# Sends over 128 partitions, the last three of them aimed past the table

## The reference, cut to what matters

```
h = (x @ W).reshape(n, 4, 64);  hl = sum(a_l * h);  hr = sum(a_r * h)
e = leaky_relu(hl[row] + hr[col]);  ee = exp(e - e_max[row])
att = ee / segment_sum(ee, row)[row];  out_h = segment_sum(att * h[col], row)       # row = src, col = dst
msgs = (x[src] @ rel_W[r]) where edge_type == r;  agg = segment_sum(msgs, dst)
out  = relu(x @ self_W + self_b + agg / deg)
```

## Time and profile before

| | |
|---|---|
| median of 3 runs | 1883.29 us (1882.06 to 1884.16) |
| span of the profiled execution, first to last instruction | 1879.7 us |
| PE, DVE, ACT, POOL busy | 76%, 66%, 32%, 70% of the span |
| sends of sort a (L761) | 102, 130.2 us busy |
| sends of sort b (L771) | 136, 167.7 us busy |
| gathers of both graph layers (L946) | 904, 862.2 us busy |

### The profile page before, as it was taken

How to read it: one execution, slowest core, us unless ns; L and a number is a source line. 1 busy time by engine, 2 the same in 40 slices (tenths; PEclk the granted TensorE clock), 3 DMA queues, 4 the chain that set the end, 5 groups by cost and what they waited for, 6 DMA issues and landing times.

```text
span 1879.7 us, 23044 instructions
## 1 busy us (share of the span) xinstructions
PE 1421.9 (76%) x6382; PEld 962.6 (51%) x6382; DVE 1234.0 (66%) x2879; ACT 608.8 (32%) x1757; POOL 1319.1 (70%) x1331
## 2 busy tenths in 40 slices
PE   5566567778888888679999966666666667786993
PEld 3333245655665555558876434444334333375992
DVE  6999977788898887868524125454444444477655
ACT  0688511136666665143332310000000000025435
POOL 0688677777777777768886747777777777714566
PEclk9799778889999999889999988988977776756996
DMA  5011144445544444310202574333333333305456
GB/s 98 10 30 32 19 106 108 107 104 134 143 121 118 122 117 107 107 44 10 58 2 66 140 227 114 107 105 106 106 104 106 105 106 106 104 26 147 149 154 187
DMA packets 110954, 186.08 MB, mean 99 GB/s; under 512 B 31578, under 2 KB 78125, under 8 KB 110701
## 3 DMA queue, kind: packets, MB, share of 16 engines
q0 software_dynamic: 56480, 134.84, 28.0%
q1 hardware_dynamic: 54349, 49.75, 9.4%
HBM read 152.80 MB, written 31.43 MB: 98 GB/s over the span
## 4 chain that ended last, share of the span: by engine, by line
POOL 37%; PE 23%; DVE 19%; issue 13%; DMA 8%; DVEq 0%; ACT 0%; POOLq 0%; SPq 0%; ACTq 0%
POOL gath L946 30%; PE ps L992 6%; DVE hot_c L675 6%; DMA gath<-y_tab,index_b 6%; POOL slot_tab_b L771 5%; PE ps L1482 4%; PE ps L1920 3%; PE ps L1931 3%; DVE hot_r L666 2%; DMA gath<-h_tab,index_a 2%; DVE acc L982 1%; DVE gath L1031 1%; PE ps L1656 1%; DVE hot L970 1%; POOL acc L1236 1%
## 5 line engine op out<-in xcount | busy, mean ns | idle before, releaser
L992 PE MATMUL ps<-gath,hot 128*125 128x260 f32 (+1 forms) x1808 | 595.4, 469 | 297.5 <-DVE gath L1031 99.1
L992 PEld LDWEIGHTS ps<-gath,hot 128*125 128x125 f32 x1808 | 364.3, 221 | 487.4 <-DMA gath<-y_tab,index_b 196.3
L946 POOL DMA_INDIRECT gath<-h_tab,index_a x464 | 446.2, 962 | 146.8 <-issue 136.2
L946 POOL DMA_INDIRECT gath<-y_tab,index_b x440 | 416.0, 945 | 154.9 <-issue 119.4
L982 DVE TENSOR_TENSOR acc<-acc,ps 125x257 f32 (+1 forms) x672 | 284.5, 423 | 316.6 <-PE ps L992 277.7
L716 PE MATMUL ps<-hot_c,pay 125*128 125x440 f16 (+1 forms) x901 | 194.6, 367 | 61.6 <-ACT pay L699 61.6
L771 POOL DMA_INDIRECT slot_tab_b<-sent_word_b,sent_to_b x136 | 167.7, 1233 | 36.3 <-issue 36.3
L761 POOL DMA_INDIRECT slot_tab<-sent_word,sent_to x102 | 130.2, 1277 | 81.7 <-DVE sent_to L514 50.9
L699 ACT ACTIVATE pay<-hot_r,plan_b 125x128 f16<-125x128 f16 x578 | 172.0, 386 | 0.0
L716 PEld LDWEIGHTS ps<-hot_c,pay 125*128 125x128 f16 x901 | 87.5, 100 | 160.6 <-ACT pay L699 81.5
L1031 DVE TENSOR_TENSOR gath<-gath,ps 128x1024 f32<-128x1024 f32 x116 | 136.0, 1214 | 0.0
(11 more groups left out here) (360 smaller groups left out, 2034.4 us busy)
## 6 DMA issues: line engine op xcount, KB each, us to landing
y_tab<-ybuf SPq DMA_DIRECT2D x25, 448.0 KB
y_slots<-y_buf SPq DMA_DIRECT2D x64, 128.0 KB, 1.9
gath<-h_tab,index_a POOLq DMA_INDIRECT x464, 2.8
gath<-y_tab,index_b POOLq DMA_INDIRECT x440, 2.8
h_tab<-hbuf SPq DMA_DIRECT2D x25, 113.8 KB
xa<-in_x SPq DMA_DIRECT2D x1, 2800.0 KB
xa<-in_x SPq DMA_DIRECT2D x5, 560.0 KB
xn_tab<-acc SPq DMA_DIRECT2D x5, 560.0 KB
```

The lines of the kernel that those rows point to most:

```text
L946: p.indirect_dma_start(gath[:, ring(k) + s, 0:width], None, table, bass.IndirectOffsetOnAxis(ap=index[g][:, col:col + 1], axis=0)).then_in ...
L992: ins = t.matmul(sum_p(g, q, width), hot[:, s, :], gath[:, s, 0:width], start=(e == 0), stop=(e == n - 1))
```

## The change

All four tiles get 128 partitions. Ahead of the first use GpSimd writes 0 over the words and 2^20 over the targets, in all 128 partitions; VectorE then fills partitions 0 to 124 as before, so that partitions 125 to 127 keep the target 2^20. Each send covers 128 partitions and carries a bound, the last index of its table (59391 or 56319). An index above the bound is skipped, without an error. The number of sends and their order stay.

```
+NOWHERE = 1 << 20
-    sent_word = low.tile("sent_word", [NP, SENT])
-    sent_to = low.tile("sent_to", [NP, SENT], I32)
+    sent_word = low.tile("sent_word", [128, SENT])
+    sent_to = low.tile("sent_to", [128, SENT], I32)
...
-    sent_word_b, sent_to_b = (mid.tile(n, [NP, SENT_B], I32) for n in ("sent_word_b", "sent_to_b"))
+    sent_word_b, sent_to_b = (mid.tile(n, [128, SENT_B], I32) for n in ("sent_word_b", "sent_to_b"))
...
         p.memset(ones_b[:, :], 1.0)
+        for word, to in ((sent_word, sent_to), (sent_word_b, sent_to_b)):
+            p.memset(word[:, :], 0)
+            p.memset(to[:, :], NOWHERE)
         p.memset(prefix["a"][:, 0:1], 0.0)
         p.memset(zeros_e[:, :], 0.0).then_inc(pool_ready, 1)
...
-        v.tensor_tensor(sent_word[:, :], low_bits[:, EC - SENT:], high_bits[:, EC - SENT:], ALU.mult)
-        v.scalar_tensor_tensor(sent_to[:, :], plan["a"][:, 0, EC - SENT:], float(COLS), plan["a"][:, 1, EC - SENT:], ALU.mult, ALU.add
+        v.tensor_tensor(sent_word[0:NP, :], low_bits[:, EC - SENT:], high_bits[:, EC - SENT:], ALU.mult)
+        v.scalar_tensor_tensor(sent_to[0:NP, :], plan["a"][:, 0, EC - SENT:], float(COLS), plan["a"][:, 1, EC - SENT:], ALU.mult, ALU.add
...
             p.indirect_dma_start(slot_tab, bass.IndirectOffsetOnAxis(ap=sent_to[:, c:c + 1], axis=0),
-                                 sent_word[:, c:c + 1], None).then_inc(s_gath[c % RING], 16)
+                                 sent_word[:, c:c + 1], None, bounds_check=128 * COLS - 1, oob_is_err=False).then_inc(s_gath[c % RING], 16)
...
             p.indirect_dma_start(slot_tab_b, bass.IndirectOffsetOnAxis(ap=sent_to_b[:, c:c + 1], axis=0),
-                                 sent_word_b[:, c:c + 1], None).then_inc(s_gath[slot], 16)
+                                 sent_word_b[:, c:c + 1], None, bounds_check=128 * COLS_B - 1, oob_is_err=False).then_inc(s_gath[slot], 16)
```

More of the change, by code:

```diff
@@ L530, in finish_sent @@
     def finish_sent(v):
-        v.scalar_tensor_tensor(sent_word_b[:, :], oth_f["b"][:, EC - SENT_B:], 128.0, local_f[:, EC - SENT_B:], ALU.mult, ALU.add)
-        v.scalar_tensor_tensor(sent_to_b[:, :], plan["b"][:, 0, EC - SENT_B:], float(COLS_B), plan["b"][:, 1, EC - SENT_B:], ALU.mult, ALU.add
+        v.scalar_tensor_tensor(sent_word_b[0:NP, :], oth_f["b"][:, EC - SENT_B:], 128.0, local_f[:, EC - SENT_B:], ALU.mult, ALU.add)
+        v.scalar_tensor_tensor(sent_to_b[0:NP, :], plan["b"][:, 0, EC - SENT_B:], float(COLS_B), plan["b"][:, 1, EC - SENT_B:], ALU.mult, ALU.add
                                ).then_inc(words_ready, 1)
```

## The result

The kernel with the change takes 1865.65 us in the median of 4 runs (1863.93 to 1866.42), the kernel before 1882.87 us (4 runs, 1882.06 to 1884.16): a ratio of 0.9905, with an interval of 0.9893 to 0.9917. Direction and mechanism came out as forecast; the size didn't. The profiled executions differ by a little less, 1879.7 and 1864.6 us of span: 15.1 us.

A forecast was written before the change was run, and what follows sets the result against it. VectorE alone was taken to bound sort a, slowed by sends, with PE covering most of sort b. Memsets +0.6, VectorE's relief -9.0 and sort b -0.8 summed to -9.2 us: 1874.1 us, range 1867 to 1888.

The forecast's parts named there:

- The send: GpSimd's sends: 17 fewer rounds of descriptors to each engine shorten a send from 1187 to 946 ns.
- rival A: Sends: they get no shorter, or their hold-up of VectorE stays; 1883.4 us, chance 0.27.
- VectorE's relief: Sort a: column one-hots get back time lost beside sends, 9.0 us between bounds of 0 and 13.4.
- two thirds: Sort a: share taken of the 13.4 us that VectorE could get back, giving 9.0 us.
- upper bound of 13.4: Sort a: VectorE's gain in us if sends held it up only as gathers do, 0.043 us each.
- rival C: Sort a: full relief of VectorE, 13.4 us and more; 1869.7 us, with no stall some 3 less; chance 0.12.
- The memsets: Kernel start: four memsets ahead of VectorE's first instruction add 0.6 us, all on the path.
- Sort b: Feed-forward layer: shorter sends remove PE's wait for ACT, -0.8 us; `hi_b` keeps its place on SP, 0.
- B: Sends: the bound costs more than the rounds save, so the kernel is slower; 1898 us, chance 0.13.
- All behind sort a is one chain: Slots, gathers and sums after sort a move as a whole, so its gain reaches the end.

The follow-up runs named there:

- run 11: Kernel before, sends of sort a covering only 124 partitions, no bound or memsets, left-out words not sent: 1898.05 us.
- run 12: Kernel before, sends of sort a covering only 120 partitions, no bound or memsets, left-out words not sent: 1864.88 us.
- run 9: Changed kernel with eight one-element GpSimd memsets ahead of each send of sort a: 1875.11 us.
- run 10: Kernel before with four one-element GpSimd memsets ahead of each send of sort a: 1889.15 us.
- run 13: Kernel before with the change in sort a alone, on a chip of normal speed: 1863.57 us, ratio 0.9905.
- run 14: Kernel before with the change in sort b alone, at normal speed: 1877.47 us, ratio 0.9986.
- run 15: Changed kernel with eighteen one-element GpSimd memsets ahead of each send of sort a: 1934.44 us.
- run 16: Changed kernel with its four memsets moved behind the increment that VectorE's first instruction waits for: 1863.63 us, ratio 0.9909.
- runs 1 to 8: Eight follow-up runs of the changed kernel, variants and parts, on two chips where the kernel before took 2158 to 2161 us: 2162.73 to 2285.12 us.
- run 3: Kernel before with the change in sort a alone, on a slow chip: 2237.31 us, ratio 1.0348.
- run 4: Kernel before with the change in sort b alone, on a slow chip: 2196.64 us, ratio 1.0164.
- run 5: The changed kernel itself, measured again beside the kernel before on a slow chip: 2276.68 us, ratio 1.0534.

## Why the forecast failed in size

**The send.** Right in mechanism: 17 words fewer to an engine, 213 ns less. Forecast 946 ns, measured 974; some 7 of the 28 ns are the bound (967 without it), the other 21 are the send against the gather. Runs 11 and 12 vary the words to an engine with direction and kernel held, which no row of before did; the direction, which had no row of its own, is worth no more than those 21 ns. The Trainium skill, DMA: Bandwidth & Descriptors (Anatomy of one DMA), by which generating descriptors is small, stood behind rival A; the runs differ with it, 194 ns between 25 and 8 words at nearly the same data. The Trainium skill, Perfetto Trace Analysis (DMA Instruction — SWDGE (GPSIMD)) says that such an instruction of GpSimd is shown as ending when the last descriptor is written and not when the data have moved; the trace agrees: the changed kernel's sends of sort a are listed with 974 ns, and their median from issue to landing is 2.1 us.

**VectorE's relief: the step that failed.** "I take two thirds: 9.0 us" of an upper bound of 13.4. Measured are 16.1 us between the first and the last one-hot of sort a, 18 steps of about 0.9. The mechanism was right, and this term of the sum was mis-sized: it was too small by 7.1 us, in three pieces. (1) The shading to two thirds, 4.4 us: it had no row behind it, only the thought that one-hots without gaps would be broken into more. (2) The rest that stays. The upper bound left 0.043 us to each of 73 sends, the gathers' figure, 3.1 us; the excess that is left is (396 - 392) ns x 305 = 1.2 us. That is 1.9 us more. (3) The remaining 0.8 us lie outside the column one-hots, in the row one-hots and the first steps, which the sum didn't hold. The prediction came near the right number in rival C, "no stall at all some 3 us less", 1866.7 us, with a chance of 0.12 for all of C.

Why nearly the whole hold-up goes can be read in single instructions. Before: a send from 101.70 to 102.88, and the one-hots of 102.28 and 102.89:

```profile
101.70 1.18 POOL L761 DMA_INDIRECT slot_tab<-sent_word,sent_to  x1 [0.30 <-issue]
...
102.28 0.69 DVE L675 TENSOR_SCALAR hot_c<-iota_c,plan_a 125x464 bf16<-125x464 f16 x1
...
102.89 0.38 DVE L675 TENSOR_SCALAR hot_c<-iota_c,plan_a 125x464 bf16<-125x464 f16 x1
```

And the four one-hots that start in 101.7 to 102.9, then in the changed kernel its send and its four one-hots at the same place:

```profile
L675 DVE TENSOR_SCALAR hot_c<-iota_c,plan_a x4: 381/390/685, 101.7 to 102.9; 125x464 bf16<-125x464 f16 x4
```
```profile
102.06 0.97 POOL L765 DMA_INDIRECT slot_tab<-sent_word,sent_to  x1 [0.30 <-issue]
```
```profile
L679 DVE TENSOR_SCALAR hot_c<-iota_c,plan_a x4: 381/391/426, 102.1 to 103.1; 125x464 bf16<-125x464 f16 x4
```

Only the one-hot that starts 0.58 us into the send is stretched, and it ends at 102.97, just behind the send's end at 102.88; those that start earlier in the send pass in 390 ns. In the changed kernel the stretched one takes 426 ns and again ends just behind its send.

This holds for every send of sort a of ordinary length in the traces of before, of the changed kernel and of runs 9 to 16. A column one-hot that starts in the first 0.35 us of a send takes at most 396 ns. One that starts 0.54 to 0.66 us into it ends 0.07 to 0.11 us behind the send's end, however long the send is. So a send shuts VectorE out in its last part alone, and all that a send is longer lies in that part. Run 11's column one-hots, then run 12's (57 to 190 us):

```profile
L675 DVE TENSOR_SCALAR hot_c<-iota_c,plan_a x239: 376/390/792, 60.8 to 189.8; 125x464 bf16<-125x464 f16 x120
L675 DVE TENSOR_SCALAR hot_c<-iota_c,plan_a x277: 375/390/468, 60.9 to 189.9; 125x464 bf16<-125x464 f16 x139
```

The stretched ones take 0.43, 0.45, 0.65 and 0.78 us in the mean beside sends of 974, 993, 1187 and 1317 ns (changed, run 12, before, run 11). Runs 11 and 12 changed nothing but the partitions that a send covers, and with them its length, so this is shown: what a send gets shorter, VectorE gets back nearly ns for ns, and 0.04 us are left of 0.26. That is why two thirds were too few.

Four column one-hots pass from one send's end to the next one's, in every such stretch that they fill alone, in before, the changed kernel and runs 9 to 12. They take 1.240 us, and what is over is lost: intervals of 1.279, 1.298, 1.415, 1.492, 1.545 and 1.623 us (changed; runs 12, 9; before; runs 10, 11) less 1.240 are 0.04, 0.06, 0.18, 0.25, 0.31 and 0.38 us, and the steps rise with them: 7.81, 7.88, 8.18, 8.71, 8.68 and 9.11 us. Only before and run 10 stand the wrong way round, by 0.03. The interval alone doesn't set the number, or five would pass in run 11's 1.623 us. What would set it is how long VectorE is free from a send's end to the last part of the next: GpSimd pauses 0.31 us between two sends in run 11, as in before, and 0.98 us in run 15, where five pass. This fits all seven kernels but was made from them, and where the last part begins is known only to lie between 0.35 and 0.54 us into a send.

The other direction counts in the step too. One send of a step starts while a row one-hot is under way and is stretched by it (to 2.08 us in run 9, 1.69 in run 15); a row one-hot that starts 0.3 us or more into a send leaves it at its length. (A send of 1.27 us in before and one of 1.40 in run 11 are 0.08 us long for another reason, which isn't shown.) From then on the two engines run in lockstep: a step of the changed kernel is six sends, 5 x 1.28 + 1.42 = 7.82; run 9 five, 4 x 1.415 + 2.52 = 8.18; run 11 five, 3 x 1.62 + 1.71 + 2.53 = 9.10; before eleven for two steps, 9 x 1.493 + 1.575 + 2.405 = 17.42, 8.71 each. Counted in sends, two steps went from eleven sends to twelve shorter ones. The Trainium skill, SBUF — State Buffer (Who interferes with whom), has an exclusive lock for a whole instruction in both directions. Runs 15 and 16 agree that it goes both ways. The length doesn't agree: by the rule the one-hots that start early in a send would wait as well, and they pass.

**The memsets.** 0.6 us forecast, 0.57 at the start; 0.76 at the first one-hot. Right. Run 16 shows that they would not be free behind the increment either.

**Sort b.** -0.8 us forecast; the wait is gone with it (runs 13 and 14) and `hi_b` stayed in its place on SP, its load at 1082.21, 16.0 us earlier with the rest. The mechanism is right, the total of that half is known only to within 0.8 to 4.3 us by run 14, and runs 13 and 16 put it near nothing.

**The sum with measured terms.** +0.76 - 16.1 - 0.8 is -16.1, and 15.1 are measured; the longer gathers are the only loss that was found between. In run 13, with gathers of 946 ns, the profiled span is 16.7 us under before's, which is from another chip; the medians on its own chip are 16.4 us apart. Those 3 ns change from kernel to kernel without a pattern that was found.

**The rivals.** A fell: the send is shorter and its hold-up went with it. B fell: the bound is worth 3 to 14 ns. C came nearest, and its price was still 4 us too high. "All behind sort a is one chain" held: -15.3 at the first gather, -15.1 at the end.

**Open.** What stood still on the chips of runs 1 to 8, and why it costs tens of microseconds in the stage where the sends are short, of either sort (runs 3 and 4), isn't settled. The kernel of run 3 shows nothing of it on the chip of run 13, and neither does the changed kernel on the chip of the result. Why four column one-hots pass where five would fit (run 11), and what part the largest divisor has apart from the words, are open too.

## What to carry to other kernels

Look at the bytes per packet of GpSimd's scattered sends: 125 and 124 partitions made packets of 25 and 31 words here, 128 and 120 packets of 8. Padding to 128 with targets beyond a bound made a send 213 ns shorter, the 3 to 14 ns of the bound included. Where GpSimd's DMAs run beside an unbroken series on VectorE, compare the step with the same step when GpSimd is quiet, and take the whole difference as what is at stake: shortening the sends gave back 16.1 us, where a shading to two thirds without a row gave 9.0. Time such a change on more than one chip: the same kernel was 0.9% faster on the chip of the result and 5% slower on that of run 5. An instruction moved from ahead of a wait to behind it isn't hidden when it and the waiting engine shut each other out (run 16: 0.03 of 0.57 us came back).

## What was not expected of the hardware

124 partitions make a slower send (1317 ns) than 125 (1187) or 128 (967). A send holds VectorE up only in its last part, from somewhere between 0.35 and 0.54 us on, and is itself stretched up to 1.1 us by a row one-hot, until the two loops lock into whole numbers of sends per step. Memsets of one element, 28 ns apart, hold a column one-hot up by 0.28 us; four of 102 to 136 columns and hrl's held two VectorE instructions to 0.83 us and 0.76 us, where they take 0.30 and 0.22.
